# Windowed attention in a six-layer kernel: scores and value products by blocks of 32 queries and 64 keys

## The reference

```python
def attn_layer(x, Wqkv, qs, ksc, Wo):
    qkv = x @ Wqkv                      # 128 -> 3 * 1024
    q = l2norm(q) * qs;  k = l2norm(k) * ksc
    q = q * cos * scale + rotate_half(q) * sin * scale
    k = k * cos * inv + rotate_half(k) * sin * inv
    out = local_attention(q, k, v)      # windows of 32
    return out @ Wo                     # 1024 -> 128

def local_attention(q, k, v):           # b, h, n, d; nw = n // 32
    bk2, bv2 = look(bk), look(bv)       # a window's keys: the window before and its own, 64
    mask = (it < jb) | (it > jb + w) | (jb == -1)
    sim = where(mask, -max, einsum('bhwie,bhwje->bhwij', bq, bk2) * 8)
    return einsum('bhwij,bhwje->bhwie', softmax(sim, -1), bv2)
```

## Time and profile before

| | us |
|---|---|
| median of 3 runs | 2109.58 (2108.05 to 2110.93) |
| the profiled execution | 2105.7 |
| its span, first to last instruction | 2103.9 |
| busy: PE, PEld | 1906.2 (91%), 1444.0 (69%) |
| busy: POOL, ACT, DVE | 1665.0 (79%), 1596.2 (76%), 1582.6 (75%) |
| mean granted TensorE clock | 0.973 of full |

### The profile page before, as it was taken

One profiled execution on the slowest core, in us unless ns is written; L12 is line 12 of the kernel. 1 busy time (PEld: TensorE's weight loads), 2 busy tenths in 40 slices (PEclk: granted clock), 3 DMA queues, 4 the chain that ended last, 5 costly groups with the idle time before them and its releaser, 6 DMA issues.

```text
span 2103.9 us, 67397 instructions
## 1 busy us (share of the span) xinstructions
PE 1906.2 (91%) x22192; PEld 1444.0 (69%) x22192; DVE 1582.6 (75%) x4006; ACT 1596.2 (76%) x5607; POOL 1665.0 (79%) x1252
## 2 busy tenths in 40 slices
PE   5992899998999998899989899988999998999986
PEld 3661678774777774777774677774777774777772
DVE  4766788876788876788876788876788876888865
ACT  4871788885888884888874888884888875888872
POOL 2123999985999976899976899976899976999960
PEclk9995999999999999999999999999999999999998
DMA  2001222110321111211111311111211111112110
GB/s 64 14 12 51 79 50 56 45 46 11 99 51 45 45 46 31 83 48 45 45 46 28 84 50 45 45 46 35 81 46 45 45 46 36 47 45 56 49 29 21
DMA packets 44547, 99.43 MB, mean 47 GB/s; under 512 B 7344, under 2 KB 24208, under 8 KB 43504
## 3 DMA queue, kind: packets, MB, share of 16 engines
q1 hardware_dynamic: 44400, 97.59, 17.8%
HBM read 19.59 MB, written 1.05 MB: 10 GB/s over the span
## 4 chain that ended last, share of the span: by engine, by line
PE 70%; issue 12%; POOL 8%; ACT 5%; DVE 4%; POOLq 0%; DVEq 0%; DMA 0%; ACTq 0%; SPq 0%
PE bank L1124 9%; PE bank L1137 8%; PE bank L1151 7%; PE bank L1172 7%; PE bank L1117 7%; PE bank L1153 6%; PE bank L1158 6%; PE bank L1152 6%; PE bank L1108 3%; ACT kT L525 2%; POOL rn L321 2%; POOL ropeL L358 2%; POOL tsum L323 2%; PE bank L1164 2%; PE bank L1255 2%
## 5 line engine op out<-in xcount | busy, mean ns | idle before, releaser
L321 POOL TENSOR_TENSOR rn<-n2c,half_neg 128x8 f32<-128x8 f32 x384 | 636.4, 1657 | 81.8 <-DVE n2c L793 81.0
L487 ACT ACTIVATE prob<-bank,nmax 128x96 f32<-128x96 f32 x1536 | 501.2, 350 | 130.6 <-DVE nmax L743 130.4
L323 POOL TENSOR_TENSOR tsum<-tc_,ts_ 128x512 f32<-128x512 f32 x384 | 489.3, 1274 | 0.0
L326 POOL TENSOR_TENSOR w_nat<-tsum,rn 128x512 f32<-128x512 f32 x384 | 400.6, 1043 | 37.8 <-POOL tsum L323 15.1
L786 DVE TENSOR_REDUCE n<-nat 128x8 f32<-128x512 f32 x384 | 262.3, 683 | 138.2 <-ACT nat L503 126.8
L487 ACT ACTIVATION_READ_ACCUMULATOR prob<-bank,nmax 128x1 f32 x1536 | 331.4, 216 | 0.0
L743 DVE TENSOR_REDUCE nmax<-bank 128x4 f32<-128x384 f32 x384 | 196.1, 552 | 153.7 <-PE bank L1117 146.5
L496 ACT ACTIVATE pT<-bank 96x512 f32<-96x512 f32 x384 | 230.3, 600 | 74.6 <-PE bank L1124 72.4
L1151 PE MATMUL bank<-w_hi,xs 128*128 128x512 f32 x576 | 275.1, 478 | 12.6 <-DVE ts_ L796 9.7
L796 DVE TENSOR_TENSOR ts_<-bank,ropeL 128x256 f32<-128x256 f32 x768 | 285.8, 414 | 0.0
L1124 PE MATMUL bank<-idf,prob 128*96 128x128 f32 x1536 | 245.9, 284 | 42.9 <-ACT kT L525 28.2
(11 more groups left out here) (126 smaller groups left out, 3331.0 us busy)
## 6 DMA issues: line engine op xcount, KB each, us to landing
vspace<-v_nat SPq DMA_DIRECT2D x96, 384.0 KB, 4.0
vspace<-v_nat SPq DMA_DIRECT2D x96, 256.0 KB, 3.4
vspace<-v_nat SPq DMA_DIRECT2D x95, 128.0 KB, 2.3
nat<-w_qkv SPq DMA_DIRECT2D x5, 1536.0 KB, 8.0
wo<-w_o SPq DMA_DIRECT2D x6, 512.0 KB, 4.0
w<-w SPq DMA_DIRECT2D x6, 341.0 KB, 3.1
shared<-w_qkv SPq DMA_DIRECT2D x1, 1536.0 KB, 7.0
w<-w SPq DMA_DIRECT2D x6, 192.0 KB, 3.1
```

Of the source, the lines that this page charges most:

```text
L321: nc.gpsimd.tensor_tensor(rn[:, r, :], n2c[:, r, :], half_neg[:, 0:8], ALU.pow).then_inc(pool_step, 1)
L323: nc.gpsimd.tensor_tensor(tsum[:, r, :], tc_[:, r, :], ts_[:, r, :], ALU.add).then_inc(pool_step, 1)
L326: nc.gpsimd.tensor_tensor(w_nat[:, r, :].rearrange("p (h d) -> p h d", d=D), tsum[:, r, :].rearrange("p (h d) -> p h d", d=D), rn[:, r, :] ...
L487: last = nc.scalar.activation(prob[:, 4 * b + i, :], SB[b][:, i * SPAN:(i + 1) * SPAN], ACT.Exp, bias=nmax[:, p, 8 * G + 4 * b + i:8 * G + ...
```

## The change

Scores and value products go by blocks of 32 queries and the 64 keys that these can see. `scores` gives, for each of 4 blocks, a 32-column weight tile against 64 keys; the mask `mskB` has 64 keys, and so have the maxima and the exponentials. Two heads' probabilities (2 x 64 keys) lie side by side in `probs`, so that one 128x128 transpose turns both: `transpose_probs` has one group of four in each half `G`, and waits for both calls of `exps`. `weigh_values` takes 64 rows of `pT` and of `vw` for each head, by blocks, into two banks (`O2`, bank 5 and the columns behind the output product in bank 7), and `heads_out` has a product for each. `vw` holds four blocks of 64 keys for either parity of heads, on all 128 partitions, moved by ten DMAs in a tile. `project_out` of both halves follow each other after heads 3 of the next tile, and `residual(t - 1)` moves up one tile on DVE. At the end of a layer `project_out(t, 0)` comes after `transpose_out(t, 1)`. One constant mask more is loaded.

```diff
+BLOCKS, SEEN = P // WIN, 2 * WIN
...
-        vw = vspace[0:SPAN, :].rearrange("p (r h c) -> p r h c", r=2, h=2)
+        vw = vspace[:, :].rearrange("p (r w c) -> p r w c", r=2, w=BLOCKS)
...
+        probs = prob[:, :, :].rearrange("p h k -> p (h k)")[:, 0:8 * SEEN]
-        pT = sb("pT", [SPAN, 8, P])
+        pT = sb("pT", [P, 8, P])
...
+        OB, O2 = bank[5], (bank[5][:, 0:HB // 2], bank[7][:, P:P + HB // 2])
...
             def move_values(t, p, last=False):
                 at_least(eng, pv_done, t * 2 - 2)
-                eng.dma_start(vw[WIN:SPAN, p, 0, :], v_nat[0:HALF, p, :]).then_inc(v_seen[p], 16)
-                eng.dma_start(vw[:, p, 1, :], v_nat[WIN:P, p, :]).then_inc(v_seen[p], 16)
+                for b in range(2):
+                    eng.dma_start(vw[b * SEEN + WIN:(b + 1) * SEEN, p, 0, :].rearrange("p (g c) -> p g c", g=2),
+                                  four_heads(p, b, 0, WIN)).then_inc(v_seen[p], 16)
+                for w in range(1, BLOCKS):
+                    for b in range(2):
+                        eng.dma_start(vw[b * SEEN:(b + 1) * SEEN, p, w, :].rearrange("p (g c) -> p g c", g=2),
+                                      four_heads(p, b, (w - 1) * WIN, SEEN)).then_inc(v_seen[p], 16)
                 if not last:
                     at_least(eng, pv_done, t * 2)
-                    eng.dma_start(vw[0:WIN, 1 - p, 0, :], v_nat[P - WIN:P, p, :]).then_inc(v_prev[1 - p], 16)
+                    for b in range(2):
+                        eng.dma_start(vw[b * SEEN:b * SEEN + WIN, 1 - p, 0, :].rearrange("p (g c) -> p g c", g=2),
+                                      four_heads(p, b, P - WIN, WIN)).then_inc(v_prev[1 - p], 16)
...
             def exps(t, p, G, b):
-                at_least(eng, pt_full, t * 4 + (2 * G + b - 1))
+                at_least(eng, pt_full, t * 2 + G)
                 for i in range(4):
+                    h = 2 * i + b
+                    slot = 2 * (h % 4) + h // 4
...
+                        probs[:, slot * SEEN:(slot + 1) * SEEN], SB[b][:, i * SEEN:(i + 1) * SEEN], ACT.Exp,
...
+            def probs_out(t, G, at):
+                eng.wait_ge(pt_full, t * 2 + (G + 1))
+                at_least(eng, pv_done, t * 2 + (G - 1))
+                nc.scalar.activation(pT[:, 4 * G:4 * G + 4, :], RING[at][:, :].rearrange("p (h q) -> p h q", h=4),
                                      ACT.Copy).then_inc(pt_evac, 1)
...
-                    probs_out(t, 0, 0, 6)
                     if not closing:
                         square(t + 1, 2)
-                    probs_out(t, 0, 1, 4)
+                    probs_out(t, 0, 6)
                     exps(t, p, 1, 0)
                     exps(t, p, 1, 1)
...
-                        heads_T(t + 1, 1 - p, 0, 6)
-                    probs_out(t, 1, 0, 4)
+                        heads_T(t + 1, 1 - p, 0, 4)
+                        square(t + 1, 3)
+                    probs_out(t, 1, 4 if closing else 6)
...
-                        square(t + 1, 3)
                         values(t + 1, 1 - p, 1)
-                        heads_T(t + 1, 1 - p, 1, 6)
-                    probs_out(t, 1, 1, 6)
-                    heads_out_T(t, 0, 4)
+                        heads_T(t + 1, 1 - p, 1, 4)
+                    heads_out_T(t, 0, 4 if closing else 6)
...
             def heads_out(t, p, G):
-                nc.vector.tensor_tensor(
-                    o_nat[:, G, :].rearrange("p (h d) -> p h d", d=D), OB[:, :].rearrange("p (h d) -> p h d", d=D),
+                for b in range(2):
+                    h0 = 8 * G + 4 * b
+                    last = nc.vector.tensor_tensor(
+                        o_nat[:, G, b * HB // 2:(b + 1) * HB // 2].rearrange("p (h d) -> p h d", d=D),
+                        O2[b].rearrange("p (h d) -> p h d", d=D),
...
                         heads_out(t - 1, 1 - p, 1)
-                        if not (isinstance(n, int) and n == 1):
-                            residual(t - 2, n - 2)
...
                         rotary(t + 1, n + 1, 1)
+                    if not opening:
+                        residual(t - 1, n - 1)
                     maxima(t, p, 1)
...
             def scores(t, n, p, G):
                 for b in range(2):
-                    nc.tensor.matmul(SB[b][:, 0:4 * SPAN], idb[:, :].bitcast(bf16),
+                    nc.tensor.matmul(SB[b][:, 0:4 * SEEN], idb[:, :].bitcast(bf16),
...
                 for i in range(4):
-                    g, cols = 4 * G + i, slice(i * SPAN, (i + 1) * SPAN)
-                    for half in range(2):
-                        qs, ks = slice(half * HALF, (half + 1) * HALF), slice(half * HALF, half * HALF + SPAN)
+                    g, cols = 4 * G + i, slice(i * SEEN, (i + 1) * SEEN)
+                    for w in range(BLOCKS):
+                        qs, ks = slice(w * WIN, (w + 1) * WIN), slice(w * WIN, w * WIN + SEEN)
                         for b in range(2):
                             rows = slice(b * D, (b + 1) * D)
                             last = nc.tensor.matmul(SB[b][qs, cols], qT[rows, p, g, qs], kT[rows, p, g, ks],
                                                     start=False, stop=True, skip_group_check=True)
...
+            def transpose_probs(t, G, at):
+                eng.wait_ge(p_ready, t * 4 + (2 * G + 2))
                 for i in range(4):
-                    last = nc.tensor.transpose(RING[at][0:SPAN, i * P:(i + 1) * P], prob[:, 4 * b + i, :], idf[:, :])
+                    last = nc.tensor.transpose(RING[at][:, i * P:(i + 1) * P], probs[:, 2 * i * SEEN:2 * (i + 1) * SEEN],
+                                               idf[:, :])
...
             def weigh_values(t, p, G):
+                if G == 0:
+                    at_least(eng, y_free, t)
+                eng.wait_ge(v_seen[p], seen_block(t, p))
+                at_least(eng, v_prev[p], prev_block(t, p))
+                eng.sem_inc(pv_begun, 1)
                 for i in range(4):
+                    for w in range(BLOCKS):
+                        qs = slice(w * WIN, (w + 1) * WIN)
+                        for b in range(2):
+                            rows = slice(b * SEEN, (b + 1) * SEEN)
+                            last = nc.tensor.matmul(O2[b][qs, i * D:(i + 1) * D], pT[rows, 4 * G + i, qs],
+                                                    vw[rows, p, w, (4 * G + i) * D:(4 * G + i + 1) * D], start=True, stop=True,
                                                     skip_group_check=True)
...
                     transpose_heads(t, 2, 6 if opening else 4)
                     if not opening:
-                        eng.wait_ge(pt_evac, t * 4)
+                        eng.wait_ge(ot_evac, t * 2 - 1)
                         transpose_out(t - 1, 1, 6)
-                        project_out(t - 1, 0)
...
                     transpose_heads(t, 3, 4)
+                    if not opening:
+                        project_out(t - 1, 0)
+                        project_out(t - 1, 1)
+                    if not closing:
+                        project(t + 1, 1 - p, 2)
...
-                    transpose_probs(t, 0, 0, 6)
-                    if not closing:
-                        project(t + 1, 1 - p, 2)
-                    eng.wait_ge(tp_free, t * 4 + 4)
-                    transpose_probs(t, 0, 1, 4)
+                    transpose_probs(t, 0, 6)
                     scores(t, n, p, 1)
...
                     weigh_values(t, p, 0)
-                    transpose_probs(t, 1, 0, 4)
-                    if not opening:
-                        project_out(t - 1, 1)
+                    transpose_probs(t, 1, 4 if closing else 6)
...
-                        transpose_heads(t + 1, 1, 6)
-                    eng.wait_ge(pt_evac, t * 4 + 3)
-                    transpose_out(t, 0, 4)
-                    transpose_probs(t, 1, 1, 6)
+                        transpose_heads(t + 1, 1, 4)
+                    eng.wait_ge(pt_evac, t * 2 + 2)
+                    transpose_out(t, 0, 4 if closing else 6)

                 def close_layer(t, n, p):
                     gate_up(0, 0)
                     weigh_values(t, p, 1)
-                    project_out(t, 0)
                     eng.wait_ge(ot_evac, t * 2 + 1)
                     transpose_out(t, 1, 4)
+                    project_out(t, 0)
                     project_out(t, 1)
```

More of the change, by code:

```diff
@@ L32, with build @@
 COLUMN = [0, INNER, HB, 2 * INNER, INNER + HB, 2 * INNER + HB]
-def build(nc, x, Wa, ba, Wp, bp, Wqkv, Wo, scales, W1, W2, par, rope, ident, identb, mask, select, out):
+def build(nc, x, Wa, ba, Wp, bp, Wqkv, Wo, scales, W1, W2, par, rope, ident, identb, mask, mask_block, select, out):
     f32, f32r, bf16 = mybir.dt.float32, mybir.dt.float32r, mybir.dt.bfloat16
@@ L216, in prev_in, with seen_block, prev_block @@
             return t * 8 + (0 if p == 0 else 8)
+        def seen_block(t, p):
+            return 4 * seen(t, p)
+        def prev_block(t, p):
+            return 2 * prev_in(t, p)
```

(38 more changed lines are left out.)

50 lines of the change are left out of this document (24 added, 26 removed).

## The result

| | us |
|---|---|
| forecast | 2082 (2055 to 2140) |
| after, median of 4 runs | 2135.69 (2129.95 to 2138.01) |
| before, median beside it | 2109.69 |
| ratio, 95% interval | 1.012 (1.0097 to 1.0142) |
| profiled execution, its span | 2138.0, 2136.2 |

A forecast was written before the change was run, and what follows sets the result against it. Two bounds of nearly one length: GpSimd's 16.03 us a tile and a 16.44 us chain of waits through TensorE. Savings of 7 (loop), 17 (close) and 4 (first tiles), 28 us, gave 2082 us, range 2055 to 2140.

The forecast's parts named there:

- the rule of half floor, half path: Tile loop: half of the tiles sit on GpSimd's 16.03 us, half 0.1 to 0.2 above; mean 16.14 against 16.22.
- Groups of 64 records at 1.0 us: TensorE's score and value groups: 1.0 us each as 64 matmuls; scores +0.2 us, value products -0.1.
- Rival 2: TensorE's instruction feed makes score groups take 1.3 to 1.64 us; 2155 us at 1.3; chance 0.14.
- Leg A: From GpSimd's fourth rotated set to the end of the second half's scores: 4.67 us, from 3.90.
- Leg B: From the end of the second half's scores to the next tile's mask product: 6.5 us, from 7.14.
- L: Chain of waits across the other engines, Leg A to Leg C: 16.2 to 16.3 us, from 16.44.
- Leg C: From the mask product through scores, maxima, exponentials, square and sums to GpSimd's `rn`: 5.07 us, from 5.40.
- Close: End of a layer's tiles, last mask to the FFN's second gate product: 22.6 us from 25.56; 17 us in six layers.
- First tiles: A layer's first tiles, where GpSimd waits for `n2c`: 0.6 us less a layer, 4 us in six.
- Rival 3: TensorE's longer loop body no longer stays on chip, so loop turns wait for code: 2154 us; chance 0.04.
- Rival 1: GpSimd's floor in every tile: groups take 0.65 us, legs sum to under 16.0; 45 us saved, 2065; chance 0.21.
- Rival 4: Nothing moves: GpSimd's FFN chain meets the close's gain, loop stays at 16.22 us; 2106 to 2110; chance 0.11.

The follow-up runs named there:

- e1: The changed kernel with project_out(t - 1, 0) back in its old place behind transpose_out(t - 1, 1): 2089.92 us, ratio 0.9887 to the kernel before.
- b1: The kernel before with only both output products moved behind transpose_heads(t, 3): 2180.51 us, ratio 1.032 to the kernel before.
- e5: The changed kernel with transposes 0 and 2 of each probabilities group started after the first four exponentials: 2119.98 us, ratio 1.005 to the kernel before.
- e6: The changed kernel with keys' copy before values' copy, project 0 before the value product, and two transposes per group after the first exponentials: 2093.47 us, ratio 0.9911.
- g1: The changed kernel with GpSimd scaling only half of the columns, so its result is incomplete: 2078.92 us, ratio 0.9849 to the kernel before.
- b2: The kernel before with its three DMAs of values cut into ten, same bytes and places: 2106.87 us, ratio 0.9971.
- b3: The kernel before with ScalarE's keys' copy ahead of its values' copy: 2101.08 us, ratio 0.9955.
- c3: The changed kernel with project_out(t - 1, 0) back early, keys' copy first, and two transposes per group after the first exponentials: 2075.37 us, ratio 0.9825.

## Why the prediction was wrong

By the spans, and without the start, the change cost 27 us where the forecast had it save 28. Of these 55 us the loop has 37, the end of the layers' tiles 12 and the first tiles 7.

- *Which engine bounds, and the rule of half floor, half path*: right, and shown both ways (`e1`, `b1`, `e5`, `e6`; `g1` for GpSimd's share).
- *Groups of 64 records at 1.0 us*: too high. They take 0.80 on the chain, drained 0.86. Rival 2, the instruction feed at 1.3 to 1.64 us a group, is refuted. The trace stands against the 25 ns of the Trainium skill (TensorE: Matmul & The Clock Gate, "Wait — 56ns, not 53.3ns?") for tiles side by side: 0.86 / 64 is 13 ns.
- *Leg A, 4.67*: right in size, with the output products at 1.78 foreseen and measured 1.79. The forecast let this pass because it booked 0.97 of savings in B and C against it.
- *Leg B, 6.5*: **the first failed step**, 0.5 short: its terms were right in kind and three were too small. The eight exponentials were priced at their pace (eight times 0.29 us); from the first one's start to the transposes that wait for the last it is 2.6 (947.79 to 950.41), against my 2.3, since the last one's own length and the handover come on top. The projection with its handover took 0.8 (951.03 to 951.85) against 0.7. ScalarE's square, probabilities, values and keys then run in order to 953.92, as I had them, and another 0.38 passes to the mask against my 0.25. The group of four transposes that pairing heads saves stood on the path before (0.64); the wait for all eight exponentials took its place, and `e5` shows this by taking 0.3 off L when two of four transposes need not wait.
- *Leg C, 5.07*: **the second failed step**. I took the fourth exponential as what the square waits for. It was, but only just: before, the exponentials end at 926.76 and projection 0 at 926.67 (its three parts on the chain, from 925.79), and the square starts at 926.79. After, the exponentials end at 957.35, and the square starts at 957.61, behind projection 0, whose place did not move: mask, scores, value product and projection take 3.2 us from the mask's start, 3.1 before. Shorter maxima and exponentials bought nothing. ScalarE's timeline before, then after:

```profile
926.55 0.21 ACT L487 ACTIVATION_READ_ACCUMULATOR prob<-bank,nmax 128x1 f32 x1
926.79 0.60 ACT L503 ACTIVATE nat<-bank 128x512 f32<-128x512 f32 x1
```
```profile
957.61 0.60 ACT L531 ACTIVATE nat<-bank 128x512 f32<-128x512 f32 x1 [0.26 <-PE bank L1187]
```

- B and C together are 0.9 of L, 0.46 a tile: the whole error in the loop (16.14 forecast, 16.60 measured), some 41 us over 90 tiles. By the table of the stretches it is 37: +30 (tiles 2 to 13, and tile 14) for a forecast of -7.
- *Close*: forecast 2.9 a layer. From tile 15's mask to the second gate it is 23.35 after, against 25.56, where I compared. Over the six layers it is shorter by 1.8, 2.0, 2.2, 0.3, 0.6 and 1.4, 8.3 us of the 17, and up to the next layer's first tile 5.2. In the layer shown, the work behind TensorE's wait for `o_nat` runs at the lower of the two clock levels (1.2 GHz), after the change and before it. TensorE's timeline after, and the window of the two output products (granted clock 0.53):

```profile
1103.75 0.38 PE L1135 MATMUL bank<-mskB,idb 128*128 128x256 bf16 x2 [0.51 <-ACT kT L553]
...
1109.66 0.63 PE L1198 MATMUL bank<-idf,o_nat 128*128 128x128 f32 x4 [2.83 <-DVE o_nat L780]
...
1111.09 3.49 PE L1206 MATMUL bank<-oT,wo 128*128 128x128 f32 x16
...
1127.10 1.02 PE L1276 MATMUL bank<-xnT,w 128*128 128x512 f32 x2
```
```profile
1111.00:1114.50 3.50, 3.50 (x19) 3.50 (x18) 1.48 (x10) 1.60 (x9) 1.01 (x1) 0.53 0.09 24
```

  The same before, where one product stands there (1.92 us, 1.06 at the full clock), beside two groups of transposes:

```profile
1092.94 1.92 PE L1172 MATMUL bank<-oT,wo 128*128 128x128 f32 x8
```
```profile
1091.50:1095.00 3.50, 2.97 (x14) 2.97 (x15) 2.11 (x7) 1.81 (x9) 0.75 (x1) 0.58 0.00 0
```

  So in this layer the lower clock costs some 1.7 us in either kernel (before, the transposes, the product and the transposes take 3.46 us from 1092.03 to 1095.49, for 0.44 + 0.89 + 0.44 at the full clock), and takes nothing from the forecast's gain; the 0.7 that is missing lies rather where TensorE now waits 1.71 us for the second half's eight exponentials (0.53 before). What differs is how often the clock falls. Between the mask and the second gate it falls once in all six layers before; after, once in the first three, and twice, or once for twice as long, in the last three, which gained 0.3, 0.6 and 1.4. The forecast took the clock as unchanged there. In three layers of six after, and in four in `e1`, the clock falls within 2.5 us of the end of the longer wait for the exponentials; in none of the 18 layers of the kernel before, `b2` and `b3`, where that wait is 0.53, does it fall there. That the wait causes it is likely, and not shown; `b1`, with a wait of 0.53 and one of 1.33 behind it, has such a fall in two layers.
- *First tiles, -4*: +2.6. The first of the two distances is 0.4 shorter in the mean, the second 0.9 longer; what the second waits for was not followed.
- *Transfers hidden*: right. Eight DMAs took SP 5.2 us (I had 4.7), and no engine waited for one; `b2` agrees.
- *Loop code*: three instruction fetches between 900 and 1072 us, over five turns of the loop, the last at 915: the body stays on the chip. Rival 3 is refuted.
- *Rival 1's floor in every tile* is reached, but by `c3`, not by the change. Rival 4, in which nothing moves, fails too: GpSimd's waits rose from 2.3 to 7.1 us in twelve tiles.

Not tried: output product 1 back behind value product 0, as before. The change put the value product's second bank into the bank of the output product, and I judged from the code that the two would then be written and read there with nothing to order them; no run shows it.

## What to carry over

Where two bounds are nearly as long as each other, a saving in one stretch must be shown to lie on the path at its new place: ask of each instruction on the chain which of its other inputs comes next, before booking its gain. A loop of dependences that meets a full engine once in two tiles costs half its excess, and shows as a wait in every second tile; the full engine's own work then counts too, although it waits. A large product moved for tidiness is priced at its full length on the path; look for a stretch where its engine idles. And a cost found after a change, like that of the lower clock here, is looked up at the same place before it as well.

## What the runs showed of the hardware

- 64 score records of 64x32 weights against 64 columns, each with its weight load, took 0.86 us with their drain, as much as 32 of 64x64 against 96 (0.89).
- Two output products took 1.79 us at the full clock and 3.49 at a granted clock of 0.53, after a wait of 2.83 us. Before the change one took 1.06 and, after a wait of 2.90, 1.92. A wait of that length can thus cost some 1.7 us again behind it, though not every time: in `b2` the clock did not fall behind one of six waits of 2.9.
- GpSimd's product of 128x256 took 0.62 us against 1.04 for 128x512: halving the columns takes off 0.42.
- Cutting the transfers of values of a tile from three to ten cost nothing that the profile of `b2` shows (span 2104.0, before 2103.9).
